# Ten wide constant matmuls a turn, one a step, beside a recurrence on TensorE

## The chip, the cores and the metric

The kernel runs on one core of one Trainium2 chip. The metric is the device time of one execution in microseconds (us), as the median of several runs.

## The reference

The input x has shape (8, 32, 32, 64): 8 images, each 32 rows of 32 tokens with 64 channels. Eight layers follow each other, each added to what it reads (`x = x + layer(norm(x))`). The ones that run side by side in the part of the kernel that matters here are:

- two Mamba-2 blocks (a scan over each image row of 32 tokens, with a depthwise convolution of 4 taps),
- an ensemble of 8 small MLPs with batch norm, weighted by a softmax (`ffn0` below),
- two "product" layers: `log(exp(x - x_max) @ exp(log_w - w_max)) + x_max + w_max`, with a 64x64 matrix of its own for every pixel,
- a mixture of 8 experts with the top 2 taken (`mix`),
- an LSTM over the 1024 tokens, batch 8, hidden size 64 (`lstm`), the one long recurrence:

```python
i_t = sigmoid(xi_t + h @ V_i); g_t = tanh(xg_t + h @ V_c); o_t = sigmoid(xo_t + h @ V_o)
c_new = h * c + i_t * g_t
h_new = o_t * tanh(c_new)
```

- a 7x7 depthwise convolution (`conv`). The attention and the last mixture of experts come in a second part, which the change doesn't touch.

## The kernel before

**Turns.** The first part works on one image row of all 8 images at a time and is pipelined over the 32 rows. In turn i the LSTM handles row i, and the other layers handle rows before or behind it: `LAG` gives ffn0 and the product layer 0 the row i + 3, `mix` and product layer 1 the row i + 2, the Mamba blocks i + 4 and i + 5, and the convolution i - 5. The turns go from -5 to 32. The LSTM exists in turns 0 to 31, whatever has lag "ffn" in turns -3 to 28, and the convolution from turn 5 on. By the first scan of each row, turn 0 begins at 280.5 us in the profile, turn 1 at 358.2, turn 15 at 1397.7, turn 16 at 1471.2 and turn 22 at 1907.5.

**Weaving by hand.** Within a turn each engine's instruction stream is woven from generators, one for each layer. Each `yield` in a generator marks a place where others may come in between. The table `TIMES` holds one row of due times for each generator, in the order of the list given to `turns`, and `weave` goes through slots 0, 0.5, 1, ... and in each slot lets the generators go on whose due time has come, in the order of the list. The engines run their streams in order and wait for semaphores. So the order is fixed, and a late instruction holds up what stands behind it on its engine.

**The LSTM's step.** Step t has its products in slot t - 0.5. On TensorE: three products of 8 columns in f32 (L1047 to L1049; each shows as two records) once r_h of the step before is written. On ScalarE: tanh of the gates (L1058, L1060). On VectorE: a scan of 24 elements (L1072). On ScalarE again: tanh of the cell (L1063). On VectorE: the new r_h (L1077) and a second product for the next scan (L1079). Step t + 1 can begin only then.

**What stands near slots 22 to 31 on TensorE.** The transposes and 16 small products with 18 columns of each of the two product layers (L812, L823), the transposes of their results (L830), the LSTM's input products for the next row (L1023, L1025), the last transposes and output products of the Mamba blocks (L459, L465, L468), and the single transpose L1105. The next turn starts, behind its step 0, with twelve records of the convolution (L1152).

**PSUM.** psB has two halves of 512 columns (2 KB a partition each). ffn0 uses both; its last products fill them (L735, L736), and VectorE reads them in L783 (`f_big`). The product layer 0 then uses the first half alone. The second half is written again by ffn0 of the next turn. `ones3` (65x128) and `bias3` (65 rows, bf16) are constants; ffn0 and mix already multiply 512 columns of bias3 by ones3, to put their biases into PSUM (L735, L941).

Of the kernel before, what the change touches and what calls it, by code (L numbers as in the profile page):

```python
# [71 lines left out]
for _n, _r, _c in BIASES + LATE_BIASES:  # L72
# [65 lines left out]
    ),  # L138
# [30 lines left out]
def bc(ap, axis, n):  # L169

    ap = ap.unsqueeze(axis)
    shape = list(ap.shape)
    shape[axis] = n
    return ap.broadcast_to(shape)


def build(nc, x_in, pack_in, acc1_in, acc2_in, out):
    with ExitStack() as ctx:
# [6 lines left out]
        def sem(name):  # L185
            if name not in sems:
                sems[name] = nc.alloc_semaphore(name=f"{phase[0]}{name}")
            return sems[name]
# [28 lines left out]
        bias3 = ctx.enter_context(nc.sbuf_tensor("bias3", [65, NBIAS], BF16))  # L217
        ones3 = ctx.enter_context(nc.sbuf_tensor("ones3", [65, P], BF16))
# [21 lines left out]
        psB = ctx.enter_context(nc.psum_tensor("psB", [P, 2, 512], F32))  # L240
# [10 lines left out]
        def sb(name, *shape):  # L251
            return phase1.enter_context(nc.sbuf_tensor(name, list(shape), F32))
# [32 lines left out]
        f_big = sb("f_big", P, J, E, C);  # L285
# [33 lines left out]
        def settle(eng):  # L319

            eng.sem_inc(sem("apart"), 1)
# [480 lines left out]
        def prod_pe(pe, i, k, ps):  # L802

            i1, c = i + 1, f"c{k}"
            yield
            pe.wait_ge(sem(c + "_e"), i1)
            if k == 1:
                pe.wait_ge(sem("x4_done"), i + 2)
            else:
                pe.wait_ge(sem("x2_done"), i1)  # L810
            for j in range(J):
                last = nc.tensor.transpose(ps[:, 0, j * P:(j + 1) * P], c_e[k][:, j].rearrange("p d c -> p (d c)"), ident)  # L812
            last.then_inc(sem(c + "_et"), 1)
            for t in range(16):
                if t % 4 == 0:
                    yield
                elif t % 2 == 0:
                    yield
                if t == 0:
                    pe.wait_ge(sem(c + "_ets"), i1)  # L820
                    pe.wait_ge(sem(c + "_acc"), i * 16 + 16)
                    settle(pe)
                last = nc.tensor.matmul(ps[0:64, 0, 0:288].rearrange("p (h b t) -> p h b t", h=2, t=16)[:, :, :, t],  # L823
                                        accb[k][:, t], c_eT[k][:, :, :, t], start=True, stop=True)
            last.then_inc(sem(c + "_mm"), 1)
            yield
            pe.wait_ge(sem(c + "_q"), i1)
            settle(pe)
            for j in range(J):
                last = nc.tensor.transpose(ps[:, 0, j * C:(j + 1) * C],  # L830
                                           c_q[k][:, j * B4:(j + 1) * B4].rearrange("p b t -> p (b t)"), ident[0:64, 0:64])
            last.then_inc(sem(c + "_qT"), 1)

        def prod_act(act, i, k, ps):
            i1, c = i + 1, f"c{k}"
            yield
            act.wait_ge(sem(c + "_mx"), i1)
            for j in range(J):
                if j:
                    yield  # L840
                last = nc.scalar.activation(c_e[k][:, j], bc(c_ln[k]["xn"][:, j], 1, 2), ACT.Exp, bias=c_mx[k][:, 1, j:j + 1])
            last.then_inc(sem(c + "_e"), 1)
            yield
            act.wait_ge(sem(c + "_et"), i1)
            for h in range(2):
                if h:
                    yield
                r = slice(64 * h, 64 * h + 64)
                last = nc.scalar.activation(c_eT[k][r, h, 0:B], ps[r, 0, 0:256].rearrange("p (b h t) -> p h b t", h=2, t=16)[:, h], ACT.Copy)
            last.then_inc(sem(c + "_ets"), 1)  # L850
            yield
            act.wait_ge(sem(c + "_qT"), i1)
            nc.scalar.activation(c_l[k][:].rearrange("p j c -> p (j c)"), ps[:, 0, 0:P], ACT.Ln).then_inc(sem(c + "_l"), 1)
# [407 lines left out]
        @block.sync  # L1261
        def _(sp):

            sp.dma_start(W[:, 0:NFIRST], pack_in[:, 0:NFIRST]).then_inc(sem("w_in"), 16)
            sp.dma_start(X[:, 0:3], x_in[:, 0:3]).then_inc(sem("x_in"), 16)
            sp.dma_start(W[:, NFIRST:], pack_in[:, NFIRST:]).then_inc(sem("w_late"), 16)
            sp.dma_start(X[:, 3:], x_in[:, 3:]).then_inc(sem("x_late"), 16)
            acc_load(sp, 0, 0, acc1_in)
            acc_load(sp, 0, 1, acc2_in)
            turns(sp, lambda i, par: [  # L1270
                ("post", lambda n: x6_store(sp, n)),
                ("mix", lambda n: acc_next(sp, n, 1, acc2_in)),
                ("ffn", lambda n: acc_next(sp, n, 0, acc1_in)),
                ("block1", lambda n: mamba_sp(sp, n, 1)),
                ("block0", lambda n: mamba_sp(sp, n, 0))], lambda: None)
            sp.wait_ge(sem("x6_out"), NT * 32)
# [177 lines left out]
        @block.tensor  # L1454
        def _(pe):
            def mixed(i):

                last = i + LAG["mix"]
                return (min(last, NT - 1) if isinstance(i, int) else last) + 2

            pe.wait_ge(sem("setup"), 1)
            turns(pe, lambda i, par: [
                ("lstm", lambda n: lstm_pe(pe, n, par)),
                ("conv", lambda n: conv_pe(pe, n, par)),
                ("edge", lambda n: edge_pe(pe, n)),
                ("post", lambda n: post_pe(pe, n, mixed(i))),
                ("xproj", lambda n: xproj_pe(pe, n, mixed(i), 1 - par)),
                ("mix", lambda n: mix_pe(pe, n)),
                ("mix", lambda n: prod_pe(pe, n, 1, psC)),
                ("ffn", lambda n: ffn0_pe(pe, n)),  # L1470
                ("ffn", lambda n: prod_pe(pe, n, 0, psB)),
                ("block1", lambda n: mamba_pe(pe, n, 1)),
                ("block0", lambda n: mamba_pe(pe, n, 0))], lambda: pe.wait_ge(sem("late"), 1))

# [620 lines left out]
```

## Time and profile before

| | us |
|---|---|
| median of 3 runs | 3159.26 |
| lowest and highest | 3159.11, 3162.25 |
| span of the profiled execution | 3157.1 |
| TensorE busy in it | 2771.7 |
| VectorE busy | 1953.5 |
| ScalarE busy | 1668.0 |
| mean granted TensorE clock | 0.822 of 2.4 GHz |

The span is from the first to the last instruction of the one profiled execution. The granted clock reads 1.00 at 2.4 GHz and 0.50 at 1.2 GHz; a value between them is a stretch with some of each. The ends of matmuls are modelled, so the start of the next instruction tells more than the busy time. In the view by stretch the columns are: the stretch and its length, then busy time and instructions of TensorE's matmuls, its weight loads, VectorE, ScalarE and GpSimd, then the mean granted clock, the DMA share and GB/s. In a timeline the number in front of the engine's name is its length in us and the one before that its start, and for merged ones (x8) the length from the first start to the last end.

### The profile page before, as it was taken

What the parts mean: (1) busy time and instruction counts of PE and PEld (TensorE: products, weight loads), DVE (VectorE), ACT (ScalarE), POOL (GpSimd) and SP (SyncE); (2) the same over time, 40 slices, a digit from 0 to 9 for tenths busy, and PEclk for the clock granted to TensorE, in tenths of its full rate; (3) what the DMA queues carried; (4) which work ended last, traced back from release to release, by engine and by line L of the source; (5) the groups of instructions that cost most, each with busy time, mean ns of one, the idle gap of its engine ahead of it and who ended that gap; (6) DMA issues with size and microseconds to landing.
All of it is one profiled execution on the core that took longest, in us unless ns stands there. A gap on an engine that the chain in (4) does not pass through costs nothing. (4 is left out here: it accounts for less than half of the span.)

```text
span 3157.1 us, 64810 instructions
## 1 busy us (share of the span) xinstructions
PE 2771.7 (88%) x22240; PEld 2231.2 (71%) x22240; DVE 1953.5 (62%) x8535; ACT 1668.0 (53%) x5755; POOL 874.9 (28%) x1499
## 2 busy tenths in 40 slices
PE   4477888899999999999999999999998787887667
PEld 3366666678888788888888888788777564555556
DVE  5466666676667677777766667677754324555454
ACT  1245555566666666666665666666654423443333
POOL 2233222233233333323333333333311000000444
PEclk8677766688888888888888888888886688998888
DMA  2000000000000100000000000000000001000000
GB/s 100 14 17 18 18 19 19 19 19 19 21 21 20 32 19 19 19 19 19 19 19 19 21 21 25 27 19 19 19 17 9 3 2 28 1 1 1 8 10 11
DMA packets 54039, 59.12 MB, mean 19 GB/s; under 512 B 26576, under 2 KB 45136, under 8 KB 53328
## 3 DMA queue, kind: packets, MB, share of 16 engines
q1 hardware_dynamic: 53712, 54.99, 6.0%
q8 instruction: 177, 2.90, 0.4%
q14 instruction: 150, 1.23, 0.1%
HBM read 42.37 MB, written 4.19 MB: 15 GB/s over the span
## 5 line engine op out<-in xcount | busy, mean ns | idle before, releaser
L1072 DVE TENSOR_TENSOR_SCAN r_c<-r_wk 64x24 f32<-64x24 f32 x1024 | 244.3, 239 | 490.4 <-ACT r_wk L1058 486.5
L1058 ACT ACTIVATE r_wk<-psL 64x16 f32<-64x16 f32 x1024 | 189.1, 185 | 678.1 <-PE psL L1048 659.9
L1152 PE MATMUL psL<-img,dg 128*128 128x128 f32 x2646 | 452.7, 314 | 0.0
L1047 PEld LDWEIGHTS psL<-r_h,lv 128*64 128x64 f32 x2048 | 235.6, 162 | 291.1 <-DVE r_h L1077 162.9
L1047 PE MATMUL psL<-r_h,lv 128*64 128x8 f32 x2048 | 324.6, 231 | 80.6 <-DVE r_h L1077 74.8
L1152 PEld LDWEIGHTS psL<-img,dg 128*128 128x128 f32 x2646 | 378.4, 215 | 11.8 <-issue 3.9
L1049 PE MATMUL psL<-r_h,lv 128*64 128x8 f32 x2048 | 326.4, 232 | 0.0
L1048 PE MATMUL psL<-r_h,lv 128*64 128x8 f32 x2048 | 304.7, 222 | 0.0
L1077 DVE SCALAR_TENSOR_TENSOR r_h<-r_wk,r_tc 64x8 f32<-64x8 f32 x1024 | 196.3, 192 | 115.0 <-ACT r_tc L1063 101.5
L1063 ACT ACTIVATE r_tc<-r_c 64x8 f32<-64x8 f32 x1024 | 215.5, 210 | 83.8 <-DVE r_c L1072 37.7
L1048 PEld LDWEIGHTS psL<-r_h,lv 128*64 128x64 f32 x2048 | 252.7, 171 | 0.0
L1079 DVE SCALAR_TENSOR_TENSOR r_wk<-r_h,r_c 64x8 f32<-64x8 f32 x1024 | 223.8, 219 | 35.5
L1049 PEld LDWEIGHTS psL<-r_h,lv 128*64 128x64 f32 x2048 | 232.2, 160 | 0.0
L678 POOL TENSOR_TENSOR a_xw<-a_S,a_dtm 128x512 f32<-128x512 f32 x128 | 150.5, 1204 | 188.1 <-DVE a_dtm L591 188.1
L1060 ACT ACTIVATE r_wk<-psL 64x8 f32<-64x8 f32 x1024 | 181.7, 177 | 24.7
L929 PE MATMUL psC<-m_xT,W 128*128 128x256 f32 x512 | 167.3, 421 | 0.0
L451 PE MATMUL psA<-a_xw,a_RM 128*32 128x64 f32 x2048 | 133.1, 230 | 18.8 <-DVE state L628 17.2
L755 ACT ACTIVATE f_h<-psB,bn0b,bn0s 128x256 f32<-128x256 f32 x256 | 132.7, 556 | 8.1 <-PE psB L720 5.9
L669 POOL TENSOR_TENSOR a_bc<-W,a_S 128x128 f32<-128x128 f32 x128 | 49.5, 407 | 309.0 <-DVE a_S L565 302.0
L451 PEld LDWEIGHTS psA<-a_xw,a_RM 128*32 128x32 f32 x2048 | 113.5, 116 | 30.2 <-issue 25.9
L944 PEld LDWEIGHTS psC<-W,m_h 128*128 128x128 f32 x1024 | 130.2, 193 | 1.8
L823 PE MATMUL psC<-c_eT,accb 128*64 128x18 f32 x1024 | 129.5, 273 | 0.0
(376 smaller groups left out, 6558.8 us busy)
## 6 DMA issues: line engine op xcount, KB each, us to landing
accb<-acc_in SPq DMA_DIRECT2D x64, 512.0 KB, 4.3
a_xy<-a_E SPq DMA_DIRECT2D x512, 16.0 KB, 1.8
W<-pack_in SPq DMA_DIRECT2D x1, 3165.0 KB, 13.7
x6d<-X SPq DMA_DIRECT2D x64, 32.0 KB
out_x<-X SPq DMA_DIRECT2D x32, 64.0 KB, 1.6
X<-x_in SPq DMA_DIRECT2D x1, 1856.0 KB, 17.7
W<-pack_in SPq DMA_DIRECT2D x1, 1331.0 KB, 5.8
X<-x_in SPq DMA_DIRECT2D x1, 192.0 KB
```

Source lines behind the costliest of these rows:

```text
L451: last = nc.tensor.matmul(bk[TT * j:TT * j + TT].rearrange("p (b h d) -> p h b d", b=B4, h=NH)[:, h], u["RM"][:, j * NH + h], u["xw"][:, j ...
L929: last = nc.tensor.matmul(psC[:, e // 2 % 2, (e % 2) * 256:(e % 2 + 1) * 256], w128("m1w1", e * P, (e + 1) * P), u["xT"][:], start=True, s ...
L1047: nc.tensor.matmul(psL[0:64, par, c:c + LB], lv[:, 0], h, start=False, stop=False, skip_group_check=True)
L1048: nc.tensor.matmul(psL[0:64, par, c + LB:c + 2 * LB], lv[:, 1], h, start=False, stop=False, skip_group_check=True).then_inc(sem("r_z"), 1)
L1049: nc.tensor.matmul(psL[64:P, par, c:c + LB], lv[:, 2], h, start=False, stop=False, skip_group_check=True).then_inc(sem("r_zo"), 1)
L1058: nc.scalar.activation(o, psL[0:64, par, c:c + 2 * LB].rearrange("p (g b) -> p g b", b=LB), ACT.Tanh).then_inc(sem("r_gi"), 1)
L1060: nc.scalar.activation(TO, psL[64:P, par, c:c + LB], ACT.Tanh)
L1063: nc.scalar.activation(r_tc[:], r_c3[:, t % 2, 2::3], ACT.Tanh, scale=0.5).then_inc(sem("r_tc"), 1)
L1072: v.tensor_tensor_scan(r_c3[:, t % 2, :], r_wk[:, 0:24], r_wk[:, 30:54], 0.0, ALU.mult, ALU.add).then_inc(sem("r_c"), 1)
L1077: v.scalar_tensor_tensor(r_h[0:64, t + 1], TO, 1.0, r_tc[:], ALU.add, ALU.mult).then_inc(sem("r_hr"), 1)
L1079: v.scalar_tensor_tensor(r_wk[:, 32:56:3], r_h[0:64, t + 1], 0.5, r_c3[:, t % 2, 2::3], ALU.mult, ALU.mult).then_inc(sem("r_hc"), 1)
L1152: last = nc.tensor.matmul(o, dg[:, ky * KT + kx], rows[:, :, ky, kx:kx + IMG], start=(n == 0), stop=(n == KT * KT - 1))
```

## The change

TensorE gets one more generator, `pulse_pe`, between product layer 0 and Mamba block 1, and one more row in its table. It issues ten matmuls, one in each of the slots 22.5 to 31.5, in every turn that has ffn0 (turns -3 to 28). Each multiplies the constants ones3 (as weights, 65x128) by 512 columns of bias3 (bf16) and writes the second half of psB. Before the first of them TensorE waits until both f_big products of VectorE (L783) of this turn are done. Nothing reads what they write.

```diff
         (20.5, 21.5, 21.5, 23, 23, 23, 23, 24, 24, 27.5),
+        (22.5, 23.5, 24.5, 25.5, 26.5, 27.5, 28.5, 29.5, 30.5, 31.5),
...
+        def pulse_pe(pe, i):
+
+            for n in range(10):
+                yield
+                if n == 0:
+                    pe.wait_ge(sem("f_big"), 2 * i + 2)
+                nc.tensor.matmul(psB[:, 1, :], ones3[:], bias3[:, 0:512], start=True, stop=True)
...
                 ("ffn", lambda n: prod_pe(pe, n, 0, psB)),
+                ("ffn", lambda n: pulse_pe(pe, n)),
                 ("block1", lambda n: mamba_pe(pe, n, 1)),
```

Within its slot a new product comes behind the LSTM's and the product layers' work and ahead of the Mamba blocks'.

## Rows read from the trace of the kernel before

**Rows 1.** The page: busy time and share; granted clock in 40 slices, in tenths.

```profile
PE 2771.7 (88%) x22240; PEld 2231.2 (71%) x22240; DVE 1953.5 (62%) x8535; ACT 1668.0 (53%) x5755; POOL 874.9 (28%) x1499
...
PEclk8677766688888888888888888888886688998888
```

**Rows 2.** Busy time by stretch: about turn -3, then turns 1, 15, 22.

```profile
66.00:140.00 74.00, 36.73 (x246) 28.58 (x245) 42.91 (x136) 15.81 (x51) 24.16 (x37) 0.71 0.02 4
...
358.20:435.20 77.00, 66.94 (x514) 53.20 (x514) 50.78 (x240) 45.50 (x168) 23.54 (x42) 0.70 0.07 19
...
1397.70:1471.20 73.50, 71.84 (x613) 59.49 (x614) 51.22 (x240) 45.79 (x170) 23.53 (x42) 0.85 0.07 20
...
1907.50:1979.40 71.90, 69.89 (x613) 57.67 (x613) 51.11 (x239) 45.71 (x168) 23.55 (x42) 0.88 0.07 21
```

**Rows 3.** The same view, around the clock's fall in turn 15.

```profile
1448.40:1451.80 3.40, 2.78 (x32) 2.21 (x30) 2.02 (x13) 2.25 (x10) 1.13 (x3) 1.00 0.10 24
1451.80:1475.20 23.40, 22.99 (x159) 18.81 (x160) 14.26 (x76) 13.24 (x55) 5.18 (x13) 0.50 0.19 54
```

**Rows 4.** TensorE's timeline, end of turn 15; idle before in brackets.

```profile
1456.04 0.25 PE L1047 MATMUL psL<-r_h,lv 128*64 128x8 f32 x1
...
1456.47 1.02 PE L823 MATMUL psC<-c_eT,accb 128*64 128x18 f32 x8
1457.56 0.28 PE L1047 MATMUL psL<-r_h,lv 128*64 128x8 f32 x1
...
1462.83 0.45 PE L830 MATMUL psC<-W,c_q 64*128 64x64 f32 x2 [0.17 <-DVE c_q L875]
...
1464.35 1.22 PE L1023 MATMUL psL<-r_xT,lua 65*128 65x256 f32 x2
1465.50 1.12 PE L1025 MATMUL psL<-r_xT,lub 65*64 65x256 f32 x2
...
1469.16 1.22 PE L465 MATMUL psA<-a_T,wout 128*128 128x256 f32 x2
1470.32 0.28 PE L1047 MATMUL psL<-r_h,lv 128*64 128x8 f32 x1
...
1470.85 2.93 PE L1152 MATMUL psL<-img,dg 128*128 128x128 f32 x12
```

**Rows 5.** VectorE's timeline there: the writes of r_h ahead of those L1047.

```profile
1455.35 0.16 DVE L1077 SCALAR_TENSOR_TENSOR r_h<-r_wk,r_tc 64x8 f32<-64x8 f32 x1
...
1457.35 0.16 DVE L1077 SCALAR_TENSOR_TENSOR r_h<-r_wk,r_tc 64x8 f32<-64x8 f32 x1
...
1469.97 0.16 DVE L1077 SCALAR_TENSOR_TENSOR r_h<-r_wk,r_tc 64x8 f32<-64x8 f32 x1
```

**Rows 6.** TensorE's timeline in turn 16: steps 22, 23 and 24, high clock.

```profile
1523.92 0.22 PE L1047 MATMUL psL<-r_h,lv 128*64 128x8 f32 x1 [0.37 <-DVE r_h L1077]
...
1525.26 0.22 PE L1047 MATMUL psL<-r_h,lv 128*64 128x8 f32 x1 [0.25 <-DVE r_h L1077]
...
1526.77 0.22 PE L1047 MATMUL psL<-r_h,lv 128*64 128x8 f32 x1 [0.17 <-DVE r_h L1077]
```

**Rows 7.** Lengths: timelines, the view of L465 (min/median/max), the page (L823).

```profile
1417.36 0.38 PE L735 MATMUL psB<-bias,ones 65*128 65x512 bf16 x1
1417.58 0.83 PE L736 MATMUL psB<-W,f_h 128*128 128x128 f32 x6
...
1426.09 1.02 PE L929 MATMUL psC<-m_xT,W 128*128 128x256 f32 x4
...
526.05 2.93 PE L720 MATMUL psB<-f_xT,W 128*128 128x256 f32 x6
...
L465 PE MATMUL psA<-a_T,wout x64: 634/688/796, 50.0 to 2268.6; 128*128 128x256 f32 x64
...
L823 PE MATMUL psC<-c_eT,accb 128*64 128x18 f32 x1024 | 129.5, 273 | 0.0
```

**Rows 8.** The view of f_big, turn 15: ns, then first and last start.

```profile
L783 DVE TENSOR_TENSOR f_big<-psB,f_w x2: 675/676/676, 1424.5 to 1428.9; 128x512 f32<-128x512 f32 x2
```

## The prediction

> **What bounds the kernel now.** I read the page first: TensorE is the busiest engine and its granted clock is below full in most slices [rows 1]. A busy share says little here, since the ends of matmuls are modelled, so I went to the stages. The main loop is 37 turns, and 32 of them carry 32 steps of a recurrence: three small TensorE products (L1047 to L1049), a tanh on ScalarE, a scan on VectorE, another tanh, and the new r_h (L1077), which the next step's products wait for. All other layers are woven between these steps. Busy time by turn gives 77.0 us for turn 1 at a mean clock of 0.70, 73.5 us for turn 15 at 0.85, and 71.9 us for turn 22 at 0.88 [rows 2]. So the clock is worth something.
>
> Within turn 15 (1397.7 to 1471.2) the clock is 1.00 until about 1451.8 and 0.50 from there to 1475.2, some way into the next turn [rows 3]. That low stretch covers steps 23 to 31, just where the ten new products go. So the first question is whether a product per step keeps the clock up. The second is who sets the pace of these steps if it doesn't.
>
> For the pace I set TensorE's timeline beside VectorE's. Where the recurrence sets the pace, L1047 starts 0.06 us after r_h is written: r_h starts at 1457.35 and takes 0.16, so it is there at 1457.51, and L1047 starts at 1457.56 [rows 4, 5]. Where TensorE sets it, L1047 comes later. At step 25 r_h is there at 1455.51 and L1047 starts at 1456.04, 0.53 us late. At the next turn's step 0 r_h is there at 1470.13 and L1047 starts at 1470.32, 0.19 late [rows 4, 5]. At 1.2 GHz TensorE is thus the bound, or nearly, of most of the steps 23 to 31.
>
> **What the change adds.** One generator with ten steps in 32 turns (turns -3 to 28): 320 matmuls of 65 rows by 512 columns in bf16, each with a 65x128 weight load. Nothing is removed, and nothing else is moved. Nobody reads the result.
>
> The one wait costs nothing: it asks for both f_big products of VectorE, and the last of these starts at 1428.9 and takes 0.68 us [rows 8], more than 22 us ahead of the first new product (behind L1047 of step 23). If that cover were gone, every later matmul of the turn would queue behind it, the recurrence's among them. Of the other engines none waits for anything new. So all the cost is TensorE's own time.
>
> **The price of one product.** The same shape exists already: at the high clock L735 starts at 1417.36 and its successor at 1417.58, so it holds the engine 0.22 us. An f32 record of 256 columns holds it as long: L929 has four in 1.02 us, and with the last one's own length of about 0.38 off (L735's, as wide) that is (1.02 - 0.38) / 3 = 0.21. At the low clock six such records (L720) take 2.93 us, and with one's own length of 0.63 off (L465's shortest) (2.93 - 0.63) / 5 = 0.46 [rows 7]. No bf16 product of this width is shown at the low clock. The bounds are 0.43 (twice 0.21) and 0.59 (L465 at the low clock, each with a full f32 weight load: two in 1.22 us, so 1.22 - 0.63 between their starts [rows 4, 7]). I take 0.45, since the new product's weights are bf16 and its load at the high clock is hidden.
>
> **Where it lies.** I go through the ten places with the low clock:
> - 1st, behind step 23: in turn 16 the clock is still high there and L1047 of step 24 has an idle gap of 0.17 us before it plus the modelled tail, so 0.22 is covered [rows 6]. In turn 15 it is low and TensorE-bound. One turn in three is of that kind: 0.15 on average.
> - 2nd: the next L1047 is 0.53 late already, so all of it: 0.45.
> - 3rd and 4th: the eight L823 records from 1456.47 last 1.02 us, of which 0.27 is the last one's own length [rows 4, 7]. So they start (1.02 - 0.27) / 7 = 0.11 apart, the last at 1457.22, and the engine could go on at 1457.33. L1047 starts at 1457.56, which leaves 0.23 idle. Each costs 0.45 - 0.23 = 0.22.
> - 5th: twelve L823 records in place of eight; no gap is left: 0.45.
> - 6th: the transposes L830 wait 0.17 us for VectorE [rows 4], which hides that much: 0.28.
> - 7th to 10th: L1047 is late without them (0.19 at step 0 [rows 4, 5]), with L1023 and L1025, L459 and L465 in front. All of it: 4 x 0.45 = 1.80. The tenth stands directly before step 0 of the next turn, and twelve convolution products follow there, so nothing gives it back.
>
> The sum is 3.57 us a turn. It is paid in the 29 turns that have both the recurrence and the products (0 to 28): 103.5 us. In the three turns before them TensorE has room, 36.7 us busy of 74.0 in the first [rows 2], so most of it lies in idle time. The bounds are 0 and 3 x 4.5 = 13 us; I take 3, as half of the time and more is idle there.
>
> **What the clock gives back if it stays low.** The clock rises in the run of convolution products behind step 0, twelve records in 2.93 us [rows 4]. The ninth and tenth product stand before that run, so the rise may come earlier in some turns. Turn 22, whose mean clock is 0.03 above that of turn 15, is 1.6 us shorter [rows 2]. I take a fifth of that, 0.3, in the 24 turns that have both the convolution and the products: -7 us. The whole is +103.5 + 3 - 7 = +99.5. The profiled span of 3157.1 becomes 3256.6. The median of the runs lies 2.2 above that span, so it is 3259.
>
> **Does the clock stay high?** The rows speak against it. From 1448.4 to 1451.8 TensorE does parts of two recurrence steps, conv and transposes and eight L823 records, with 32 records and 2.78 us busy, and the clock falls right behind [rows 3]. The new products come two to three recurrence steps' work later, when only L823 and the recurrence are left, and bring one wide product for every 1.5 us. In the low stretch L1023 and L1025 follow each other from 1464.35 to 1466.62 without a gap [rows 4], more solid work than the new products bring to any such stretch, and the clock stays at 0.50 [rows 3]. It returns only behind the twelve L1152 records, which end at 1473.8.
>
> Here a rule of the skill speaks the other way. The Trainium skill, page "TensorE: Matmul & The Clock Gate", section "Why this matters for your kernels", says to leave no gap of TensorE above about 3 us between bursts if the high clock is to be kept. The trace does not agree that this is enough: the recurrence's products come every 1.5 us and the clock falls all the same. By the rule read as "more matmuls, no fall" the sum would be that of the first rival.
>
> **The rivals.**
> - *The products hold the clock (faster).* For it: they are the only wide products in these steps. Against it: the paragraph before the last one. Its price: a step at the high clock goes from L1047 to L1047 in 1.34 us (1523.92 to 1525.26 [rows 6]) against 1.52 at the low one (1456.04 to 1457.56 [rows 4]), and steps that TensorE bounds lose their lateness. Steps 24 to 31 and step 0 gain 9 x 0.18 = 1.6. The lateness of step 25 (0.53) and of steps 31 and 0 (0.19 each, taking step 31 as step 0) goes: 0.9. L1023 and L1025 take 2.3 us at the low clock and save about 1.0 of it at the high one. That is 3.5 us in all. The products (0.22 each) fit into the gaps. 29 x -3.5 = -101 us, so about 3058. It decides from the point at which the clock is still 1.00 at steps 24 and 25. Chance 0.12.
> - *TensorE's lateness is apparent and the products lie in idle time.* For it: modelled ends. Against it: L1047's start against r_h does not rest on ends of matmuls. At 0.5 us or less a turn it gives 3159 to 3174. Chance 0.06: 0.04 for no change, 0.02 for up to 3174.
> - *The clock falls elsewhere too.* A turn of another length meets the clock's changes in other places. Turn 1, with a mean clock of 0.70, is 77.0 us long, and turn 15 with 0.85 is 73.5 [rows 2]. If ten turns go that way, that adds 10 x 3.5 = 35 us to the forecast: 3294, and for all 24 turns 3343. Chance 0.10.
> - That the products are not run is excluded: their generator stands in the list, and the wait is met.
>
> **How the numbers follow.** The forecast (low clock kept, products paid) has 0.72. Its own range: with 0.59 each instead of 0.45 a turn pays 1.4 us more (29 x 1.4 = 41), and with the warm-up turns' bound (+10) the total is 3310. With 0.43, the gap of 0.23 at each of the first six places (6 x 0.20 = 1.2, and 4 x 0.43 = 1.7: 2.9 a turn, 84 in all), nothing in the warm-up and twice the gain from an earlier rise (-14), it is 3157 + 84 - 14 + 2 = 3229. The range of 8 in 10 takes in the ten-turn case of the third rival and reaches below for a clock that rises earlier than that in most turns (1.2 us more in 29 turns, -34): 3195 to 3315. About 0.2% (6.3 us) is what a measurement of this kernel can tell from no change. Slower by more than that: 0.72 + 0.10 + 0.02 = 0.84. No change: 0.04. Faster: 0.12.
>
> **What the profile after would show.** Each new product at the low clock has its next neighbour 0.43 to 0.59 us behind it, and ten of them a turn stand among L823, L1023 and L465. The granted clock of a turn stays near 0.85, with the fall at steps 22 to 24. Turn 15 lasts about 76.8 us and turn 1 about 80.5 (77.0 + 3.57). L1047 of steps 26 and 27 starts about 0.28 us behind r_h instead of 0.06. The prediction is wrong if the clock reads 1.00 behind step 25, or if it rises again before step 0 in most turns.

## The result, and the profile after

The changed kernel takes 3276.23 us in the median of four runs (3263.59 to 3282.98), against 3160.76 us in the median of four runs of the kernel before (3159.11 to 3167.81). The ratio is 1.0356, with a 95% interval of 1.0327 to 1.0384. So it is slower by 115.5 us. The forecast was slower by 99.5, at 3259, with a range of 3195 to 3315. Of all the executions in this document one lies far apart from the others of its kernel: the second of four of the kernel with thirty products of 65 rows took 4917.18 us, at a clock that reads 1.0; it has no trace, its cause is open, and that kernel's ratio is taken from the other three.

The profiled execution has a span of 3261.8 us, 104.7 above the span of before. It is the shortest of the four: 3263.59 us at a mean granted clock of 0.815, where the longest has 3282.98 at 0.808. Before it was 0.822. The page of the changed kernel, to be read beside [rows 1]:

```profile
PE 2904.8 (89%) x22560; PEld 2273.3 (70%) x22560; DVE 1953.5 (60%) x8535; ACT 1668.0 (51%) x5755; POOL 875.1 (27%) x1499
...
PEclk9677776688888888888888888888877688998788
```

TensorE has 133 us more of busy time and exactly the 320 new matmuls. VectorE, ScalarE and GpSimd are the same within 0.2 us. The clock's row is nearly that of before, so the clock does not stay up anywhere new.

Busy time by stretch, turns 1, 15 and 16 of the changed kernel, then the two sides of the clock's fall in turn 15 (columns as in [rows 2, 3]):

```profile
364.60:444.80 80.20, 70.72 (x524) 54.11 (x524) 50.66 (x239) 45.32 (x167) 23.55 (x42) 0.69 0.06 19
...
1451.80:1527.00 75.20, 73.66 (x623) 58.90 (x623) 51.16 (x240) 45.71 (x169) 23.55 (x42) 0.86 0.07 20
1527.00:1603.20 76.20, 75.42 (x623) 60.38 (x623) 51.15 (x239) 45.72 (x168) 23.55 (x42) 0.84 0.07 19
...
1505.30:1508.70 3.40, 3.14 (x44) 2.53 (x43) 2.56 (x15) 2.12 (x11) 0.32 (x2) 1.00 0.10 25
1508.70:1532.50 23.80, 23.80 (x141) 17.32 (x139) 12.71 (x68) 11.40 (x47) 6.12 (x15) 0.50 0.17 51
```

Turn 1 was 77.0 us long and is now 80.2. Turn 15 goes from 73.5 to 75.2 [rows 2]. Turn 16 was 72.7 long. It now takes 76.2. The clock still falls in turn 15, and from there on TensorE is busy for 23.80 of 23.80 us.

I split the two spans by the start of each turn's first scan:

| | before | after | difference |
|---|---|---|---|
| to the start of turn 0 | 280.5 | 283.0 | +2.5 |
| turns 0 to 4 | 389.7 | 403.9 | +14.2 |
| turns 5 to 26 | 1599.8 | 1680.2 | +80.4 |
| turns 27 and 28 | 135.4 | 143.5 | +8.1 |
| the rest | 751.6 | 751.2 | -0.4 |

A turn of the long middle part grows from 72.7 to 76.4 us. It now has 25.0 us at the low clock on average instead of 21.2 (turns 6 to 26), and the fall still comes at steps 22 to 24. By the length of each step, from scan to scan, in the mean of turns 6 to 26:

| step | before | after | forecast of the difference | measured |
|---|---|---|---|---|
| 23 | 1.65 | 1.92 | +0.15 | +0.27 |
| 24 | 1.98 | 2.30 | +0.45 | +0.32 |
| 25 | 1.54 | 1.94 | +0.22 | +0.40 |
| 26 | 1.54 | 1.94 | +0.22 | +0.40 |
| 27 | 1.72 | 2.37 | +0.45 | +0.65 |
| 28 | 3.85 | 3.85 | +0.28 | 0 |
| 29 | 2.31 | 2.79 | +0.45 | +0.48 |
| 30 | 1.68 | 2.03 | +0.45 | +0.35 |
| 31 | 1.68 | 2.35 | +0.90 (two products) | +0.67 |
| 1 of the next turn | 2.72 | 2.82 | 0 | +0.10 |

The other steps did not change. The whole is +3.62 (steps 23 to 31 alone +3.54), against +3.57 in the forecast.

TensorE's timeline at the end of turn 15 shows where the time lies (start, length, engine, line; the new product is L841, and a line below it is 9 further down than before, so L1056 is the L1047 of [rows 4]):

```profile
1510.30 0.61 PE L841 MATMUL psB<-bias,ones 65*128 65x512 bf16 x1
1510.84 0.28 PE L1056 MATMUL psL<-r_h,lv 128*64 128x8 f32 x1
...
1512.23 0.61 PE L841 MATMUL psB<-bias,ones 65*128 65x512 bf16 x1
1512.78 0.28 PE L1056 MATMUL psL<-r_h,lv 128*64 128x8 f32 x1
...
1521.02 0.61 PE L841 MATMUL psB<-bias,ones 65*128 65x512 bf16 x1
1521.42 0.42 PE L460 MATMUL psA<-W,a_y 128*128 128x128 f32 x1
...
1524.73 1.06 PE L466 MATMUL psA<-a_T,wout 128*128 128x256 f32 x2
1525.58 0.63 PE L841 MATMUL psB<-bias,ones 65*128 65x512 bf16 x1
1526.15 0.28 PE L1056 MATMUL psL<-r_h,lv 128*64 128x8 f32 x1
```

VectorE's timeline beside it, the writing of r_h for the first of these L1056:

```profile
1510.22 0.16 DVE L1086 SCALAR_TENSOR_TENSOR r_h<-r_wk,r_tc 64x8 f32<-64x8 f32 x1
```

The first L841 of these lines, which is the third of turn 15, starts at 1510.30, and r_h is there at 1510.22 + 0.16 = 1510.38. So the product is in TensorE when r_h arrives, and the recurrence's L1056 starts at 1510.84, 0.46 us behind r_h. Before it was 0.06 in such a step [rows 4, 5], and the forecast was about 0.28. The engine goes from L841 to L1056 in 0.54 to 0.57 us, but from L841 to L460 in 0.40.

The view of L841 (min/median/max in ns) tells at which clock its products run:

```profile
L841 PE MATMUL psB<-bias,ones x320: 389/609/634, 145.3 to 2509.1; 65*128 65x512 bf16 x160
```

In the timeline a product lasts 0.39 us where the clock is high and 0.61 to 0.63 where it is low. In turns 6 to 26 the first one is short in 18 of 21, the second in two (turns 15 and 16) and in part in a third. From the third product on all are long, in every turn.

Last, TensorE's waits from 700 to 2200 us (for what, then us in total, times, the longest in us):

```profile
PE psL L1056 <- DVE r_h L1086: 12.5, 40, 0.4
PE psB L711 <- DVE f_xn L347: 1.5, 4, 0.8
```

In these 1500 us TensorE waits 14 us, never longer than 0.8 at a time.

### The profile page after: what moved, and what is told of

It reads as the page before. It is cut to its first block and busy times, and to the rows that moved or that the text cites. A ratio compares the mean times of both kernels' runs of the same rounds, so it can differ in the third digit from the quotient of the medians.

```text
span 3261.8 us, 65450 instructions
## 1 busy us (share of the span) xinstructions
PE 2904.8 (89%) x22560; PEld 2273.3 (70%) x22560; DVE 1953.5 (60%) x8535; ACT 1668.0 (51%) x5755; POOL 875.1 (27%) x1499
## 5 line engine op out<-in xcount | busy, mean ns | idle before, releaser
L1056 PEld LDWEIGHTS psL<-r_h,lv 128*64 128x64 f32 x2048 | 235.0, 162 | 326.6 <-DVE r_h L1086 174.6
L1056 PE MATMUL psL<-r_h,lv 128*64 128x8 f32 x2048 | 325.2, 231 | 71.2 <-DVE r_h L1086 70.1
L841 PE MATMUL psB<-bias,ones 65*128 65x512 bf16 x320 | 190.2, 597 | 0.0
## 6 DMA issues: line engine op xcount, KB each, us to landing
W<-pack_in SPq DMA_DIRECT2D x1, 3165.0 KB, 14.2
```

The lines of the kernel that those rows point to most:

```text
L841: nc.tensor.matmul(psB[:, 1, :], ones3[:], bias3[:, 0:512], start=True, stop=True)
L1056: nc.tensor.matmul(psL[0:64, par, c:c + LB], lv[:, 0], h, start=False, stop=False, skip_group_check=True)
```

## The experiments

There are two questions: is the cost TensorE's time for the columns, paid at the low clock, and why can the products not hold the clock up? Each kernel computes the whole reference; what is added or moved in TensorE's stream is all that differs. A turn's length below is always the mean of turns 6 to 26 unless another is named, against 72.73 us for before.

### Eight columns in place of 512

```diff
-                nc.tensor.matmul(psB[:, 1, :], ones3[:], bias3[:, 0:512], start=True, stop=True)
+                nc.tensor.matmul(psB[:, 1, 0:8], ones3[:], bias3[:, 0:8], start=True, stop=True)
```

> The ten products stay, each with its 65x128 weight load, but are 8 columns wide in place of 512. Theory A (the cost is TensorE's time for 512 columns at the low clock, 0.43 to 0.46 us each, in steps that TensorE bounds): nearly all of the cost goes, at most 0.1 us a product is left and half of that lies in gaps, so 3160 to 3185 us, turn 15 near 73 us. Rival B (each product costs a fixed time, for its weight load and for the break it makes in the stream): the width matters little, 3230 us or more.

Measured: 3173.94 us, ratio 1.0044 (1.0028 to 1.0061). A turn takes 72.89 us, 0.16 more than before. The warm-up ahead of turn 0 is 5.3 us longer, and step 27 takes 1.95 instead of 1.72. Turn 16 of this kernel:

```profile
1475.90:1549.00 73.10, 72.18 (x623) 60.12 (x623) 51.14 (x240) 45.72 (x169) 23.54 (x42) 0.85 0.07 20
```

It has all 623 matmuls of the changed kernel at the length of a turn before. Ten more instructions with their weight loads and the wait cost 0.16 us a turn. The other 3.46 of the 3.62 are the 504 columns that are missing here. The 0.16 is a difference of two things: steps 25 to 31 are 0.32 longer, 0.23 of it in step 27, and steps 23 and 24 are 0.16 shorter, because the clock falls a step or two later in some turns.

### The first five places, and the last five

```diff
-        (22.5, 23.5, 24.5, 25.5, 26.5, 27.5, 28.5, 29.5, 30.5, 31.5),
+        (22.5, 23.5, 24.5, 25.5, 26.5),
...
-            for n in range(10):
+            for n in range(5):
```

> Only the products of slots 22.5 to 26.5, so five a turn. Theory A (each place costs on its own, by how late TensorE is there): by the steps of the changed kernel steps 23 to 27 are 2.1 us longer than before, so 29 x 2.1 = +61 us, 3220 us. By the prediction's own sum for these places (1.49 us) +43, 3203 us. Rival C (the cost is a matter of where the clock changes, so it needs all ten): no such split, for instance all of the +115 or nothing.

The second kernel keeps (27.5, 28.5, 29.5, 30.5, 31.5) instead.

> Only the products of slots 27.5 to 31.5, five a turn. Theory A: by the steps of the changed kernel steps 28 to 31 are 1.4 us longer than before and by the prediction's sum the five cost 2.08 us, so +41 to +60 us, 3201 to 3221 us. If the costs are separate, this result and that of the first five add up to the +115 us of all ten. Rival C: they don't add up, by more than 20 us.

Measured: the first five alone take 3213.91 us (ratio 1.0178, 1.0150 to 1.0205), the last five alone 3201.88 (1.0125, 1.0089 to 1.0160). A turn grows by 1.81 and by 1.78 us. The sum, 3.59, is close to the 3.62 of the ten. Step by step:
- In the first kernel steps 25 to 27 are as long as with all ten products (1.95, 1.94, 2.37), and in the second so are steps 29 to 31 (2.78, 2.03, 2.35). The first kernel leaves steps 28 to 31 as they were, and the second steps 23 to 28. So a product's cost lies where it stands.
- Steps 23 and 24 of the first kernel grow by 0.19 and 0.21, where all ten gave 0.27 and 0.32. The clock falls only at step 24 in five of its turns, and in one turn of the changed kernel.
- In the second kernel steps 1 and 2 of the next turn grow by 0.12 and 0.15, since after turns 9 and 20 the clock rises only in step 2.

The steps with products give 1.85 + 1.49 = 3.34 of the 3.54. The rest is at the clock's edges, and that the whole agrees to 0.03 is partly chance. In the medians the two add up to 53.9 + 41.9 = 95.8 us against 115.5, and this 19.7 is just inside the 20 that I had allowed. In the profiled executions they add up to 52.4 + 49.0 = 101.4 us against 104.7. So most of the 19.7 is the difference between one execution and another.

### Three products in each place, of 65 and of 128 rows

```diff
-                nc.tensor.matmul(psB[:, 1, :], ones3[:], bias3[:, 0:512], start=True, stop=True)
+                for _ in range(3):
+                    nc.tensor.matmul(psB[:, 1, :], ones3[:], bias3[:, 0:512], start=True, stop=True)
```

> Three products of 512 columns in each of the ten places, one behind the other. Theory A (the high clock goes with how much of the time TensorE streams, and one product a step is too little): with three, 0.65 us a step at the high clock, the clock stays at 1.00 through most of steps 23 to 31. The steps are then TensorE-bound at the high clock, about 1.75 us each against 1.5 to 2.3 before, so -0.5 to +1.5 us a turn: 3145 to 3205 us, mean clock above 0.90. Rival D (such products don't count for the clock, or something else than TensorE's work makes it fall): it stays low, each product costs 0.43 us or more, 12 us a turn, 3500 us.

Measured: 3536.18 us, ratio 1.1189 (1.1157 to 1.1220). I had expected thirty products to hold the clock. That failed, and the rival's number came out. All of turns 5 to 26 take 82.9 to 87.5 us, with 28 to 40 us of each at the low clock. Step 28, which one product had left alone, is now 0.77 longer. Its turn 16, and one of the triples:

```profile
1593.80:1678.50 84.70, 83.93 (x643) 63.17 (x643) 51.17 (x240) 45.82 (x169) 23.56 (x42) 0.80 0.06 18
...
1650.87 1.46 PE L842 MATMUL psB<-bias,ones 65*128 65x512 bf16 x3
```

Three starts and one end in 1.46 us, of which the last one's own length is 0.61: so (1.46 - 0.61) / 2 = 0.43 us from product to product at the low clock. Was it too little work, work of the wrong kind, or work too late? The next kernel takes the same time in TensorE but uses all 128 rows of the array. The new rows hold whatever lies there, as nobody reads the product.

```diff
-        bias3 = ctx.enter_context(nc.sbuf_tensor("bias3", [65, NBIAS], BF16))
-        ones3 = ctx.enter_context(nc.sbuf_tensor("ones3", [65, P], BF16))
+        bias3 = ctx.enter_context(nc.sbuf_tensor("bias3", [P, NBIAS], BF16))
+        ones3 = ctx.enter_context(nc.sbuf_tensor("ones3", [P, P], BF16))
...
-                nc.tensor.matmul(psB[:, 1, :], ones3[:], bias3[:, 0:512], start=True, stop=True)
+                for _ in range(3):
+                    nc.tensor.matmul(psB[:, 1, :], ones3[:], bias3[:, 0:512], start=True, stop=True)
```

All other uses are cut to rows 0 to 64, as they were.

> As the run with three products in each place, but the constants' tiles are 128 rows high and the new products use all 128 (the old bias products keep 65). TensorE's time for each is the same. Theory R (in the run with three the clock stayed low because the products use 65 of 128 rows and don't count in full): now the clock stays at 1.00 through most of steps 23 to 31, steps of about 1.75 us, 3145 to 3205 us, mean clock above 0.90. Rival D (constant bf16 products don't count, or the fall has another cause): as with 65 rows, about 3536 us at a mean clock near 0.79.

Measured: 3493.2 us, ratio 1.1065 (1.1028 to 1.1101). The median is almost as bad, so what I had expected of the rows failed as a number. But the turns are now of two kinds. Its turns 14 and 16:

```profile
1486.10:1561.80 75.70, 73.04 (x641) 56.41 (x644) 51.14 (x239) 45.72 (x168) 22.97 (x42) 0.95 0.07 20
...
1650.50:1735.70 85.20, 81.93 (x641) 61.65 (x643) 51.16 (x240) 45.84 (x169) 23.62 (x42) 0.82 0.06 17
```

Turns 5, 10, 14, 18 and 24 hold the clock up to step 29 and take about 75.7 us, with some 7 us at the low clock. The others fall as before and take 85 to 88.7. With 65 rows not one of the 22 turns held. The same kernel with two products a place:

> Two products of 128 rows in each of the ten places. Theory R leaves it open whether two are enough. If the clock holds, a step at the high clock is 1.5 us with them and the end of a turn 1.3 us shorter than before: about 3120 us. If it holds in part of the steps or turns only: 3150 to 3300. Rival D (it falls all the same): each pair costs about 0.9 us less the gaps, 7.7 us a turn, 3380 us.

Measured: 3365.77 us, ratio 1.0656 (1.0623 to 1.0689). Four turns (5, 10, 23, 26) hold and take 73.8 to 74.5 us, the others 80 to 84. Its turns 16 and 23:

```profile
1577.70:1657.60 79.90, 77.12 (x632) 59.86 (x635) 51.19 (x240) 45.83 (x169) 23.60 (x42) 0.85 0.07 19
...
2146.60:2220.50 73.90, 71.59 (x631) 56.28 (x634) 51.14 (x239) 45.72 (x168) 23.57 (x42) 0.94 0.07 20
```

The 128 rows do one thing more. In the kernel with triples of 65 rows the clock rises only 2.6 us or more behind the first convolution product of the next turn, in every one of turns 6 to 26, as in the kernel before (1.9 or more). With triples of 128 rows it rises between 0.3 us ahead of that product and 0.6 us behind it. The next turn's first convolution products start at 1763.56 in the first line, of the kernel with 65 rows, and at 1735.34 just ahead of the second, of the kernel with 128 rows:

```profile
1763.50:1766.40 2.90, 2.90 (x14) 2.67 (x13) 1.88 (x12) 1.21 (x5) 0.82 (x2) 0.50 0.00 0
...
1735.60:1738.50 2.90, 2.83 (x26) 2.50 (x25) 2.19 (x13) 1.43 (x7) 1.06 (x3) 1.00 0.00 0
```

So triples of 128 rows, with the data that they hold here, can bring the clock back in these steps.

### The same triples two steps sooner

From the kernel with three products of 128 rows:

```diff
-        (22.5, 23.5, 24.5, 25.5, 26.5, 27.5, 28.5, 29.5, 30.5, 31.5),
+        (20.5, 21.5, 22.5, 23.5, 24.5, 25.5, 26.5, 27.5, 28.5, 29.5),
```

> As the run with three products of 128 rows in each place, but the ten places stand two steps sooner, in slots 20.5 to 29.5. In that run two turns (10 and 14) kept the clock up to step 29 and are some 10 us shorter than the others, and in the others it fell at step 22 or 23, where the first products stand. Theory S (work of full height keeps the high clock but doesn't bring it back in these thin steps, so it has to be there before the fall): now the clock holds through step 29 in nearly all turns from 5 on, which then last 74 to 78 us; 3210 to 3290 us, mean clock above 0.88. Rival G (the two turns were chance, the fall comes whatever stands there): as before, about 3490 us.

Measured: 3279.0 us, ratio 1.0360 (1.0308 to 1.0411), 214 us less than two steps later, with the same instructions. The mean clock is 0.875. Now all turns from 5 to 26 hold the clock to step 29 at least, and turns 6 and 18 to their end. 9.2 us of a turn are at the low clock. Its turn 18, its turn 14, and the two sides of a fall in turn 14:

```profile
1706.70:1778.90 72.20, 71.20 (x644) 55.71 (x644) 51.04 (x239) 45.67 (x168) 23.52 (x42) 0.99 0.07 21
...
1400.90:1479.10 78.20, 76.06 (x644) 58.66 (x643) 51.23 (x239) 45.76 (x168) 22.92 (x42) 0.91 0.07 19
...
1400.90:1404.30 3.40, 2.65 (x26) 2.32 (x24) 2.73 (x17) 1.33 (x6) 1.67 (x4) 1.00 0.00 0
1404.30:1415.00 10.70, 9.80 (x49) 7.96 (x50) 6.60 (x34) 4.05 (x18) 1.74 (x5) 0.53 0.01 2
```

Turn 18 carries thirty products more than a turn before and is no longer, 72.2 us, at 0.99. But in 18 of turns 6 to 26 the clock falls again at step 1 and stays low to step 2 or 4 (step 2 takes 3.24 us in the mean against 1.72). Steps 2 to 4 are 2.5 us longer together, which is most of the turn's 3.6. So the mean turn is 76.3 us, as long as with ten products of half the rows that hold nothing (76.4). So for these triples the time at which they come decides whether the clock stays up through steps 23 to 28. What was gained in the low stretch was paid in the fillers' own time and in the new falls. My theory had a second half, that such work does not bring the clock back, and that is not so: in 18 of the turns it falls at step 29 and is back 2.0 to 2.4 us ahead of the next turn's convolution. Triples of 65 rows two steps sooner were not run, so this doesn't show that the 128 rows are needed.

### Ten steps earlier, at the high clock

```diff
-        (22.5, 23.5, 24.5, 25.5, 26.5, 27.5, 28.5, 29.5, 30.5, 31.5),
+        (12.5, 13.5, 14.5, 15.5, 16.5, 17.5, 18.5, 19.5, 20.5, 21.5),
```

> The ten products of 65 rows as in the changed kernel, but in slots 12.5 to 21.5, where the clock is high from turn 5 on. Theory A (a product costs TensorE's time where TensorE is the bound, and that is half at the high clock): 0.22 us each, all of it where convolution and expert products stand beside the recurrence, so up to 2.2 us a turn, +64 us: 3190 to 3225 us. Rival E (the price comes from the low clock alone, at the high one there is room): 3160 to 3175 us.

Measured: 3212.8 us, ratio 1.0181 (1.0135 to 1.0226). A turn grows by 1.20 us: steps 13 to 20 by 0.17, 0.22, 0.32, 0.17, 0.10, 0.32, 0.22 and 0.21, which is 1.73, and steps 23 and 24 get 0.26 and 0.18 back, because the clock falls a little later (19.3 us at the low clock instead of 21.2). The same ten products of 65 rows cost a third of what they cost in the low stretch. At the high clock one costs between 0.10 and 0.32 us, 0.22 in the mean of the eight that cost anything, which is what I had read there. The last two, in steps 21 and 22, cost nothing: there was room for them.

### The kernel's own work in the thin stretch

The convolution's products are 128 rows high, are needed anyway, and stand mostly before step 21. These kernels add nothing to the kernel before. They only move due times, in all but one of them in the convolution's row of TensorE's table alone.

```diff
-        (0, 0, 0, 0.5, 0.5, 7, 8.5, 8.5, 9.5, 10, 11, 11, 12, 13.5, 15.5, 16, 16.5, 16.5, 16.5, 18, 18, 18, 18, 18.5, 18.5, 19.5, 20, 21),
+        (0, 0, 0, 0.5, 0.5, 7, 8.5, 8.5, 9.5, 10, 11, 11, 12, 13.5, 15.5, 16, 16.5, 16.5, 18, 18, 19.5, 20.5, 21.5, 22.5, 23.5, 24.5, 25.5, 26.5),
```

> The kernel before, without new products, but with the convolution's own work spread later: of the pairs of taps due at 16.5 to 21 one a step now stands in slots 20.5 to 26.5. It is work of 128 rows in f32, four records or 0.43 us a step at the high clock. Theory A with R: it keeps the clock at 1.00 for one to three more stretches, steps 23 to 27 go at 1.5 us, and steps 17 to 21 lose what TensorE made late there: 1.5 to 2.5 us a turn in 22 to 24 turns, so 3100 to 3127 us. Rival F (the clock falls at the same place, and the moved work costs 0.85 us a step at the low clock): 2 to 3 us a turn more, 3200 to 3230 us.

Measured: 3251.28 us, ratio 1.0289 (1.0239 to 1.0339). Slower, and again with two kinds of turns, here 16 and 17:

```profile
1484.20:1555.00 70.80, 68.78 (x613) 56.38 (x613) 50.98 (x239) 45.79 (x168) 23.60 (x42) 0.91 0.07 21
1555.00:1633.30 78.30, 76.53 (x613) 63.11 (x613) 51.09 (x240) 45.88 (x169) 23.60 (x42) 0.81 0.07 19
```

Ten turns (6, 7, 9, 11 to 13, 15, 16, 24, 25) hold the clock to steps 26 to 28 and take 70.7 to 73.8 us. In eleven it falls at steps 20 to 22, at or just behind the steps that lost products, and they take 77.8 to 78.4. Turn 19 lies between, with the fall at step 23 and 75.7 us. Two tries to mend that, one denser from 18 on and one later as a whole (which also moves three more due times behind it, two of the LSTM's input products on TensorE and one of the convolution's eviction on ScalarE):

```diff
+        (0, 0, 0, 0.5, 0.5, 7, 8.5, 8.5, 9.5, 10, 11, 11, 12, 13.5, 15.5, 16, 18, 19, 20, 21, 21.5, 22, 22.5, 23.5, 24, 25, 26, 26.5),
```

> Convolution spread again, no new products, but without a hole at the steps where the clock falls: of the pairs of taps due at 16 to 21 eleven now stand in slots 18 to 26.5, at least one a step and two in steps 22 and 24. In the first spread the clock held to step 27 in some turns (about 71 us long) and fell at step 22 in others (about 78). Theory S: now all turns from 5 on are of the first kind, 70.5 to 71.5 us against 72.7, and the result is 3159 - 22 x 1.7 = 3115 to 3140 us. Rival G: turns of both kinds remain, 3200 us or more.

```diff
+        (0, 0, 0, 0.5, 0.5, 7, 8.5, 8.5, 9.5, 10, 11, 11, 12, 13.5, 18, 20, 21, 21.5, 22.5, 23.5, 24.5, 25.5, 26.5, 27, 27.5, 28, 28.5, 29.5),
```

> As the last one, but the convolution reaches slot 29.5, its eviction is due at 30 and the LSTM's input products for the next row at 30.5 in place of 28.5. Theory S: the clock holds through step 29 or to the end of the turn, 2 to 3 us a turn below the kernel before: 3090 to 3120 us. Rival H (the convolution, its eviction and the input products now stand one behind the other at the end of the turn and the recurrence waits): 1 to 4 us a turn above it, 3190 to 3280 us, whatever the clock.

Measured: 3341.93 us (1.0553, 1.0515 to 1.0592) and 3461.17 us (1.0948, 1.0930 to 1.0966). Both are misses. Turn 11 of the first in two stretches, and turn 16 of the second whole:

```profile
1149.10:1197.00 47.90, 46.49 (x402) 38.96 (x402) 36.67 (x163) 30.33 (x104) 18.95 (x30) 0.93 0.01 2
1197.00:1231.60 34.60, 34.43 (x212) 28.13 (x213) 14.55 (x77) 15.49 (x66) 4.59 (x12) 0.50 0.14 41
```

```profile
1600.80:1686.20 85.40, 83.42 (x613) 69.13 (x613) 51.24 (x240) 45.83 (x169) 23.57 (x42) 0.72 0.06 17
```

In the first the clock falls at steps 18 to 22 in 21 of the 22 turns; in the second at step 17 in every turn. Each time the fall comes at the steps from which work was taken away, or up to four steps behind them, and the products that follow, the moved ones among them, don't bring the clock back before the next turn. They run at half speed. So I took the products for the thin stretch from everywhere and left no hole:

```diff
+        (0, 0, 0, 0.5, 0.5, 8.5, 10, 11, 12, 13.5, 15.5, 16, 16.5, 18, 18.5, 19, 19.5, 20, 20.5, 21, 21.5, 22.5, 23.5, 24, 24.5, 25.5, 26, 26.5),
```

> The kernel before with the convolution spread more evenly, nothing added: pairs of taps are taken from the densest steps too (slots 7 to 11 lose four), and slots 18.5 to 26.5 hold one at least in each step and two in most, so that the steps 19 to 22, where the clock fell in the first two spreads, are thicker than there and not thinner. Eviction and input products stay where they are. Theory S: the clock holds from step 2 to step 27 in nearly all turns from 5 on, each as long as the good turns of the first spread (70.8 to 71.4 us) or up to 0.8 more for the pairs at steps 19 to 26, so 22 x (0.7 to 1.7) below the kernel before: 3122 to 3145 us, mean clock 0.86 or more. Rival G (a hole remains somewhere in some turns and costs those 5 us each): 3170 to 3270 us.

Measured: 3170.09 us against 3161.3, ratio 1.0021 (1.0005 to 1.0038). Turns 15 and 16 of this kernel, and then its turns 27 and 28:

```profile
1388.80:1461.00 72.20, 69.86 (x613) 57.03 (x613) 50.98 (x240) 45.61 (x169) 23.51 (x42) 0.90 0.07 21
1461.00:1532.30 71.30, 68.53 (x613) 55.97 (x613) 50.93 (x239) 45.52 (x168) 23.51 (x42) 0.93 0.08 21
...
2249.70:2327.00 77.30, 72.56 (x541) 60.90 (x541) 40.82 (x202) 41.38 (x153) 17.39 (x32) 0.74 0.06 17
2327.00:2408.80 81.80, 75.25 (x469) 62.91 (x469) 32.01 (x170) 34.83 (x135) 12.26 (x24) 0.60 0.03 8
```

Turns 27 and 28 of the kernel before:

```profile
2270.00:2337.60 67.60, 62.99 (x541) 52.79 (x541) 41.63 (x202) 41.50 (x153) 17.43 (x32) 0.85 0.07 20
2337.60:2405.40 67.80, 59.75 (x469) 49.90 (x469) 31.50 (x169) 34.77 (x134) 12.32 (x24) 0.78 0.03 10
```

In turns 5 to 26 the clock now stays up from step 2 to step 27 or 28 in each of them. Only 11.2 us a turn are at the low clock, and a turn takes 71.7 us. These 22 turns gain 23.3 us. In turns 27 and 28, where the layers that run ahead have ended, the same spreading leaves too little work at a time: the clock goes from 0.85 and 0.78 to 0.74 and 0.60, and they lose 23.7 us. The turns behind them lose another 13.3, and 3.0 go ahead of turn 0. Together that is +16.7 by the rounded parts (+16.6 in the profiled span), and +8.8 in the median. A kernel with the even row in turns 5 to 26 and the old one from 27 on was not run. As an estimate from these numbers it would be worth 23 us, 0.7%.

## Why the prediction was right

**The bound, and where the products stand.** Right. In the low stretch TensorE is the engine that others wait for, and the ten products lie on the path. The kernel with 8 columns shows that it is their columns' time, and the two halves show that it lies place by place, but for 0.2 us at the clock's edges. That rules out the rival by which they lie in idle time.

**The price of one product.** Right in size: 0.43 us from one product to the next, where I took 0.45 within 0.43 to 0.59. But it is not one number. From the product's start to the next one's it is 0.40 us ahead of the transposes and of L466, and 0.54 ahead of the recurrence's L1056 (0.57 at the tenth place). It is 0.54 ahead of L824 as well, which waits for nobody. The first group has weights of 128 columns (128*128 in the views) and the second of 64 (128*64). Why that makes a difference was not tried. The 0.54 lies within my bounds and the 0.40 just below them, and I used one value for every place.

**The single places.** Here the terms were off in both directions:
- 3rd, 4th and 5th: +0.40, +0.40 and +0.65 against 0.22, 0.22 and 0.45. The place was right, and two sizes were not: the price was 0.54, not 0.45, and the idle time was 0.13, not 0.23. The kernel with 8 columns shows the second. Its product stands 0.96 us behind the start of the eight L824, so the engine was not free 0.86 behind it, as I had worked out. Its L1056 stands 1.10 behind, where it was 1.09 before (1456.47 to 1457.56 [rows 4]). So 1.09 - 0.96 = 0.13 was idle, and 0.54 - 0.13 = 0.41. Ahead of step 27 there was no idle time, as I said, but the break in the stream costs 0.22 us even with 8 columns: from the first of the twelve to the recurrence it was 1.28, and with 8 columns it is 1.50. The rest of the 0.65 is the columns' time. The lines are the 3rd place and the 5th of the kernel with 8 columns, then the 5th of the kernel before:

```profile
1533.94 1.02 PE L824 MATMUL psC<-c_eT,accb 128*64 128x18 f32 x8
1534.90 0.19 PE L841 MATMUL psB<-bias,ones 65*128 65x8 bf16 x1
1535.04 0.27 PE L1056 MATMUL psL<-r_h,lv 128*64 128x8 f32 x1
...
1537.02 1.45 PE L824 MATMUL psC<-c_eT,accb 128*64 128x18 f32 x12
1538.40 0.19 PE L841 MATMUL psB<-bias,ones 65*128 65x8 bf16 x1
1538.52 0.28 PE L1056 MATMUL psL<-r_h,lv 128*64 128x8 f32 x1
...
1459.55 1.45 PE L823 MATMUL psC<-c_eT,accb 128*64 128x18 f32 x12
1460.83 0.25 PE L1047 MATMUL psL<-r_h,lv 128*64 128x8 f32 x1
```

- 1st: +0.27 against 0.15. I had one turn in three at the low clock and full price, and the others covered. Step 23 is wholly at the low clock in 7 of 21 turns in both kernels and is 0.45 longer there in the mean (2.49 in place of 2.04), as I had it. Where it is wholly at the high clock it takes 1.41 in place of 1.33, so the gap covered all but 0.08. But in most of the other 14 turns the fall comes within the step, and they are 0.18 longer in the mean, which I had put at nothing. The 2nd cost 0.32, not 0.45.
- 6th: 0 against 0.28. I had set it against the transposes' wait, which is the wrong cover. Step 28 waits for ScalarE, which loads two function tables of 1.28 us each there, and the delay by one product stays within these loads (with three products in this place step 28 grew by 0.77):

```profile
1516.57 1.28 ACT L862 ACT_TABLE_LOAD   x1
...
1518.33 1.28 ACT L1067 ACT_TABLE_LOAD   x1
```

- 9th and 10th: 0.67 against 0.90. The two records of L465 and what lay behind them took 1.16 us to the next L1047 before (1469.16 to 1470.32 [rows 4]). Now it is 0.85 from L466 to the product (1524.73 to 1525.58) and 0.57 from there to L1056, so 1.42 in all. That is 0.26 more, not 0.45. A part of the earlier 1.16 went to a weight load which the product now lies over. That this load is what it covers is argued from the starts, not tried.

The sum came out at 3.62 us a turn against 3.57, because these errors cancel. Single terms were wrong by up to 0.28.

**The earlier rise of the clock.** Wrong, and the largest error in the sum for the profile: I gave back 7 us, and nothing came back. A turn has more time at the low clock, not less (25.0 against 21.2 us), and step 1 is 0.10 longer. The warm-up (+2.5 against +3) and the 29 turns (+102.7 against +103.5) were near. Without the 7, the sum of the forecast would be +106.5, against +104.7 in the profile.

**From the span to the median.** I added 2.2 us, as in the profile of before. In the changed kernel the profiled run is the shortest of four, and the median lies 14.4 above its span. So 12 of the 17 us that the forecast lacks are here, and 5 in the span. Between the runs the mean clock goes from 0.815 to 0.808 while the time goes from 3263.59 to 3282.98. That may be a small share of the third rival, the clock falling in other places too. Only one of these runs has a trace, so where the others differ stays open. The price that I gave this rival, turn 1 against turn 15, compared turns of different work: turn 1 has 514 matmuls and turn 15 has 613 [rows 2].

**The clock stays low.** Right in the main. The fall stays at steps 22 to 24. But I had read in turn 15 that the products come behind the fall, and in 18 of 21 turns the first of them still starts at the high clock. One product ahead of the fall did not prevent it. In turn 15 itself the fall comes two steps later than in the kernel before, at step 24, and so it takes 75.2 us and not the 76.8 of the forecast. Three more things came out of the runs:
- Too late. In the changed kernel the clock has fallen before the third product in every one of turns 6 to 26. The triples of 128 rows take 3493.2 us in all from slot 22.5 on and 3279.0 from 20.5 on. For them it is what TensorE does ahead of the fall that holds the clock.
- Too little. With 65 rows even thirty products hold none of 22 turns; with 128 rows they hold five, and twenty of them hold four.
- Once the clock is low, the products of 65 rows do not raise it. In the changed kernel TensorE is busy for 23.80 of 23.80 us from the fall on, at 0.50. In the kernel with thirty products of 65 rows it is busy for 83.93 of 84.70 us of turn 16, and 28 us or more of each turn are low. Triples of 128 rows do raise it, by the start of the next turn's convolution at the latest, give or take 0.6 us, where it otherwise rises 1.9 us or more behind that start.

The Trainium skill, page "TensorE: Matmul & The Clock Gate", section "Why this matters for your kernels", advises to keep TensorE's gaps between bursts below about 3 us. The trace of the changed kernel does not agree that this is enough: the longest wait from 700 to 2200 us is 0.8 us, and the clock falls in every turn of them.

## What to carry to other kernels

Before filling TensorE with empty work to keep its clock up, look whether the recurrence's products start late against their input in the low stretch. If they do, every column of the filler is paid at half speed, here 0.27 to 0.65 us for a product of 512 columns, and nothing only where another engine was the bound. What held the clock in these runs stood ahead of the fall and used all 128 rows, and the kernel's own work did it most cheaply: spreading the convolution evenly gained 1.0 us a turn in 22 turns, while each spreading that left a thinner stretch behind lost up to 12.6. And an order tuned for the full pipeline needs a look at its last turns, where the same spacing has less to spread (+23.7 us in two turns here).

## What was not expected of the hardware

- Products that take the same time do not do the same for the clock. Thirty a turn of 65 rows held none of 22 turns, and thirty of 128 rows five of 22 (or all, if they start two steps sooner), and only these bring the clock back ahead of the convolution. The added rows also brought other data, and data and height were not told apart.
- One and the same program has turns of two kinds, 70.8 and 78.3 us next to each other. They have the same instructions, and what the trace shows to differ is where the clock's changes fall. Near such an edge a small edit moves the time far: two steps of due time were worth 214 us.
- The price of a product depends on what stands behind it: at the low clock 0.40 us ahead of records with weights of 128 columns, 0.43 ahead of its like, and 0.54 ahead of f32 records with weights of 64 columns. At the high clock it was 0.22 to 0.23 ahead of L813 (128 columns) and 0.32 ahead of L824 (64 columns).
